# Decoder layer on one core: low score part and logits in two 64-row tiles of TensorE, one visit per pair of heads

## What is computed

```python
# 1. square-of-relu attention to 256-row weight tables, 4 heads of 64
xn = layernorm(x, g, b)
p = square(relu(einsum('bhtd,sd->bhts', heads(xn), w_fc.reshape(-1, 64))))   # 1024 keys
x = layernorm(x + x + einsum('bhts,sd->bhtd', p, w_proj.T.reshape(-1, 64)))
# 2. cross attention, 16 heads of 16, with a bias from the fractions
Q, K, V = x @ Wq.T + bq, ctx @ Wk.T + bk, ctx @ Wv.T + bv
D = clip(frac_k - frac_q, -0.2, 0.2)
attn = gamma * Q @ K.T * 0.25 + delta * (ap[h] * max(D, 0) + an[h] * min(D, 0))
x = layernorm(x + softmax(attn) @ V @ Wo.T + bo)
# 3. one of 8 low-rank experts per token, chosen by argmax of a gate, on a shared FFN
inter = relu(x @ Wi.T + wi_b + lora_expert(x))                               # 1024 wide
x = layernorm(x + inter @ Wo2.T + wo_b)
```

## Time and profile before

| | us |
|---|---|
| median of three runs (914.18 to 917.05) | 916.64 |
| the profiled execution: its own time | 914.81 |
| its span, first to last instruction | 913.0 |
| TensorE busy | 857.1 (94%) |
| VectorE busy | 778.7 (85%) |
| ScalarE busy | 690.3 (76%) |
| GpSimd busy | 533.2 (58%) |

### The profile page before, as it was taken

How to read it: one execution, slowest core, us unless ns; L and a number is a source line. 1 busy time by engine, 2 the same in 40 slices (tenths; PEclk the granted TensorE clock), 3 DMA queues, 4 the chain that set the end, 5 groups by cost and what they waited for, 6 DMA issues and landing times.

```text
span 913.0 us, 20283 instructions
## 1 busy us (share of the span) xinstructions
PE 857.1 (94%) x7140; PEld 682.6 (75%) x7140; DVE 778.7 (85%) x2286; ACT 690.3 (76%) x1453; POOL 533.2 (58%) x620
## 2 busy tenths in 40 slices
PE   2697989999999999999999999999999999999876
PEld 1344767878878787877887787887878787788666
DVE  3869989889998998989898998989899897899842
ACT  3557889788787878878787978878797887877721
POOL 2757776666656765666666666665666565533210
PEclk9989999999999999999999999999999999999998
DMA  5223322222122223122222322212222312223000
GB/s 151 87 46 68 65 47 54 36 54 41 35 48 58 54 48 64 35 44 55 39 54 58 54 44 53 45 32 51 59 54 47 64 33 32 58 38 66 14 13 23
DMA packets 40022, 46.10 MB, mean 50 GB/s; under 512 B 10257, under 2 KB 27153, under 8 KB 39922
## 3 DMA queue, kind: packets, MB, share of 16 engines
q1 hardware_dynamic: 39922, 44.82, 24.6%
HBM read 15.42 MB, written 4.19 MB: 21 GB/s over the span
## 4 chain that ended last, share of the span: by engine, by line
PE 83%; DVE 8%; ACT 3%; issue 2%; DMA 1%; POOL 1%; SPq 0%; POOLq 0%; DVEq 0%
PE bank L218 28%; PE bank L262 12%; PE bank L343 11%; PE bank L250 7%; PE bank L334 6%; PE bank L355 6%; PE bank L251 6%; PE bank L282 2%; PE bank L404 2%; DVE bank L761 2%; PE bank L365 1%; DVE T L768 1%; DVE R L717 1%; DMA STG<-in_WvT 1%; PE bank L239 1%
## 5 line engine op out<-in xcount | busy, mean ns | idle before, releaser
L964 POOL TENSOR_SCALAR U<-DP,alph 128x512 f32<-128x512 f32 x256 | 181.5, 711 | 153.6 <-DVE NM L768 92.3
L953 POOL TENSOR_TENSOR R<-R 128x512 f32<-128x512 f32 x212 | 221.9, 1052 | 78.4 <-ACT R L496 78.4
L548 ACT ACTIVATE P<-T,NM 128x256 f32<-128x256 f32 x512 | 232.0, 508 | 3.2 <-DVE NM L768 2.7
L761 DVE SCALAR_TENSOR_TENSOR bank<-DN,alph,bank 128x512 f32<-128x512 f32 x256 | 191.9, 750 | 36.7 <-PE bank L334 35.0
L475 ACT ACTIVATE STG<-bank 128x512 f32<-128x512 f32 x256 | 152.5, 596 | 70.5 <-PE bank L343 69.1
L768 DVE CUSTOM_DVE_ANT_0 T<-bank,U 128x256 f32<-128x256 f32 x512 | 197.0, 422 | 8.8
L496 ACT ACTIVATE R<-bank 128x512 f32<-128x512 f32 x256 | 151.8, 597 | 54.4 <-PE bank L251 53.3
L343 PE MATMUL bank<-ident,P 128*128 128x128 f32 x1024 | 154.6, 273 | 5.0 <-ACT STG L475 4.8
L343 PEld LDWEIGHTS bank<-ident,P 128*128 128x128 f32 x1024 | 119.3, 140 | 24.0 <-ACT P L548 8.4
L262 PE MATMUL bank<-R,VS 128*32 128x512 f32 x1024 | 124.5, 604 | 5.5 <-DVE R L717 5.2
L250 PE MATMUL bank<-SK,KH 128*128 128x512 f32 x256 | 114.9, 449 | 8.2 <-DVE SK L711 7.6
(11 more groups left out here) (165 smaller groups left out, 1863.3 us busy)
## 6 DMA issues: line engine op xcount, KB each, us to landing
QS<-QK SPq DMA_DIRECT2D x384, 64.0 KB, 2.3
XG<-in_x SPq DMA_DIRECT2D x16, 256.0 KB, 2.7
CT<-in_ctxT SPq DMA_DIRECT2D x16, 256.0 KB, 3.6
out<-XO SPq DMA_DIRECT2D x16, 256.0 KB, 2.2
FK<-in_frac SPq DMA_DIRECT2D x16, 128.0 KB, 3.5
STG<-in_wiT SPq DMA_DIRECT2D x2, 512.0 KB, 3.5
STG<-in_woT SPq DMA_DIRECT2D x2, 512.0 KB, 4.0
STG<-in_kT SPq DMA_DIRECT2D x2, 256.0 KB, 4.0
```

What stands on the lines that cost most here:

```text
L548: eng.activation(P[n % NP][:, cs], T[n % NT][:, cs], ACT.Exp, bias=NM[:, n % 8, q:q + 1], scale=-1.0).then_inc(s_ex, 1)
L761: eng.scalar_tensor_tensor(out=L[:, :], in0=dn[:, :], scalar=alph[:, 16 + h:17 + h], in1=L[:, :], op0=ALU.mult, op1=ALU.add).then_inc(s_t1, 1)
L953: eng.tensor_tensor(r[:, :], r[:, :], r[:, :], ALU.mult).then_inc(s_sqp, 1)
L964: eng.tensor_scalar(U[n % NU][:, :], dp[:, :], alph[:, h:h + 1], 0.0, ALU.mult, ALU.add).then_inc(s_u, 1)
```

## The change

The product with the low keys (`KL`) now takes only the 64 rows of its own half that hold the high activation, and the two halves h = 0 and h = 1 stand in rows 0 to 63 and 64 to 127. The restacked queries and keys of two heads share the 128 rows (rows 0 to 47 and 64 to 111), so `QS` has half the columns, needs no zeros, and the four clearing instructions on GpSimd are gone. Such a matmul uses half of the array's rows (a 64-row tile), and the two halves write to different banks. `visit(k)` takes the place of `scores` and `logits`: it issues the high products of two score units, then the four logits matmuls of two heads, then the low products of the two units. `LEAD` = 14 sets which score units go with which heads. Both banks `pL` are filled in one visit, so a visit waits until both heads of the visit before have been read (`s_tt`, 4 * k). `head` pairs the heads so that two that stand 64 rows apart come together.

Buffers: eight `R` for six, three `U` for two, seven `STG` slots for six. `due` can shift items in the first batch (`early`) and the last (`late`), and space pairs unevenly (`gap`), and nearly all of its numbers are new.

```diff
-        NR = 6
+        NR = 8
-        QS = [sb(f"QS{i}", [128, 2, 4, 256], f32r) for i in range(2)]
+        QS = [sb(f"QS{i}", [128, 2, 2, 256], f32r) for i in range(2)]
-        NU, NT, NP, NQ = 2, 3, 3, 6
+        NU, NT, NP, NQ = 3, 3, 3, 7
         def head(n):
-            return (n % 16) // 2 + 8 * (n % 2)
+            return n % 16 // 4 * 2 + n % 2 + 8 * (n % 4 // 2)
+        LEAD = 14
-        def due(g, first, count=1, step=0, start=0):
+        def due(g, first, count=1, step=0, gap=None, start=0, early=0, late=0):
             for u in range(count):
-                b, over = divmod(g - first - step * u, PERIOD)
-                if over == 0 and start <= b < NB:
+                at = g - first - (step * u if gap is None else step * (u // 2) + gap * (u % 2))
+                b, over = divmod(at - early, PERIOD)
+                if over == 0 and start <= b <= 0:
                     yield b, u
+                b, over = divmod(at, PERIOD)
+                if over == 0 and max(start, 1) <= b < NB - 1:
+                    yield b, u
+                if at == PERIOD * (NB - 1) + late:
+                    yield NB - 1, u
-            def scores(b, u):
-                c, h = unit(u)
-                bank, before = take("sc", b, u)
-                bank_free(before)
-                pe.wait_ge(s_wlo["kT"], 1)
-                pe.wait_ge(s_skl, 2 * b + 2)
-                both = SK[:, h, :, :].rearrange("p a t -> p (a t)")
-                eng.matmul(bank[:, :], KH[:, c * 128:c * 128 + 128], both, start=True, stop=False)
-                eng.matmul(bank[:, :], KL[:, c * 128:c * 128 + 128], both, start=False, stop=True).then_inc(s_sc, 1)
+            def visit(k):
+                b, c = (k + LEAD) // 8, (k + LEAD) % 8
+                if b < NB:
+                    pe.wait_ge(s_wlo["kT"], 1)
+                    pe.wait_ge(s_skl, 2 * b + 2)
+                    for h in range(2):
+                        bank, before = take("sc", b, 2 * c + h)
+                        bank_free(before)
+                        eng.matmul(bank[:, :], KH[:, c * 128:c * 128 + 128],
+                                   SK[:, h, :, :].rearrange("p a t -> p (a t)"), start=True, stop=False)
+                if k >= 0:
+                    G, m = k // 2, k % 2
+                    pe.wait_ge(d_q[G % 2], 96 * (G // 2 + 1))
+                    pe.wait_ge(s_tt, 4 * k)
+                    for q in range(2):
+                        for j in range(2):
+                            rows = slice(64 * j, 64 * j + 48)
+                            i = eng.matmul(pL[j][:, q * 256:q * 256 + 256],
+                                           QS[G % 2][rows, 0, m, q * 128:q * 128 + 128], QS[G % 2][rows, 1, m, :],
+                                           start=True, stop=True)
+                            if q == 1:
+                                i.then_inc(s_lg, 1)
+                if b < NB:
+                    for h in range(2):
+                        own = slice(64 * h, 64 * h + 64)
+                        eng.matmul(bank_of["sc", b, 2 * c + h][:, :], KL[own, c * 128:c * 128 + 128],
+                                   SK[own, h, :, :].rearrange("p a t -> p (a t)"), start=False,
+                                   stop=True).then_inc(s_sc, 1)
-            def logits(n):
-                G, L = n // 4, pL[n % 2]
-                pe.wait_ge(d_q[G % 2], 96 * (G // 2 + 1))
-                pe.wait_ge(s_tt, 2 * (n - 1))
-                for q in range(2):
-                    i = eng.matmul(L[:, q * 256:q * 256 + 256], QS[G % 2][:, 0, n % 4, q * 128:q * 128 + 128],
-                                   QS[G % 2][:, 1, n % 4, :], start=True, stop=True)
-                i.then_inc(s_lg, 1)
...
-                for b, u in due(g, -5, 16, 39):
-                    logits(16 * b + u)
+                for b, u in due(g, -26, 8, 80, start=-2):
+                    if 8 * b + u + LEAD >= 0:
+                        visit(8 * b + u)
-                for b, u in due(g, -939, 4, 141):
+                for b, u in due(g, -931, 4, 153, early=-41, late=6):
                     av(b, u)
-                for b, u in due(g, 343, 4, 140):
+                for b, u in due(g, 293, 4, 147, early=-4, late=6):
                     values(4 * b + u)
...
-                sp.wait_ge(s_qz, 4)
                 for r, (q, k) in enumerate(((1, 2), (0, 2), (1, 3))):
                     for j in range(2):
                         p = 32 * g + 16 * j
-                        dst, src = QS[s][16 * r:16 * r + 16, :, 2 * j:2 * j + 2, :], QK[p:p + 16, q:k + 1:k - q, :, :]
+                        o = 64 * j + 16 * r
+                        dst, src = QS[s][o:o + 16, :, :, :], QK[p:p + 16, q:k + 1:k - q, :, :]
```

261 lines of the change are left out of this document (126 added, 135 removed).

## The result

The changed kernel takes 943.71 us (median of 4 runs, 942.73 to 945.09) against 916.61 before: 1.0302 times as long, 95% interval 1.0287 to 1.0318. The forecast was 929 us. The direction and the range (896 to 948) held, the size didn't: 27 us slower, not 12. The profiled execution has a span of 942.4 us and a mean granted clock of 0.982 (before 913.0 and 0.992).

The account below looks back on a forecast made before the run. TensorE sets the period. Per batch -3.8 + 4.1 + 1.4 = +1.7 us, times 12 = +20.4; other batches +1.2, start -6.5, end -1.5: span 913.0 to 926.6, forecast 929 us (1.3% slower), range 896 to 948.

Parts of the forecast that it names:

- (a): TensorE: 16 low score products and 16 heads' logits become 8 pairs each, side by side: -3.8 us per batch.
- the estimate of -2.6: Halved matmuls at 77% of ideal, from the skill's 3.07 times for four row tiles; not used in the sum.
- (b): TensorE mode changes: eight visits at 0.35 us and four more column groups at 0.32: +4.1 us per batch.
- (c): TensorE waits at `uT` for VectorE's gating after `gsT`: +1.4 us per batch, bounds 0 and 2.0.
- a sign that the prediction is wrong: TensorE at L414 was to wait over 1 us for VectorE once per batch; never waiting would refute the prediction.
- The four other batches: Batches outside the steady twelve get halved matmuls and mode changes only: +0.3 us each, +1.2 us together.
- (e): Start: batch 0's fourth `av` no longer stands behind a waiting score, and all later batches follow: -6.5 us.
- (f): End: the projection of batch 15 comes one block of 12 matmuls earlier: -1.5 us, bounds 0 and -3.
- (d): Larger rings `R`, `U`, `STG`, clearing of `QS` on GpSimd and copies in `restack`: costed at nothing.
- cheap mode changes: Rival: a visit's 64-row group costs 0.15 us, not 0.35, and new waits halve to 0.7: 897 us; chance 0.27.
- the even case: Rival: mode changes cost 4.1 us per batch but new waits only 0.3: 915 us; chance 0.13.
- the serial case: Rival: the two halves don't run side by side, so halved matmuls save 0: 984 us; chance 0.08.

Follow-up runs that it names:

- a1_full_rows: Changed kernel, same order, with logits and low products as 128-row matmuls one after the other (two heads' logits summed): 951.58 us, ratio 1.0394.
- b1_rows64: Kernel before, with each low score product reading only its own 64 rows, unpaired and in place: 998.90 us, ratio 1.0911.
- c4_start: Kernel before with three moves at the start, among them batch 0's fourth `av` ahead of batch 1's first score; no 64-row tiles: 915.77 us, ratio 0.9999.
- d1_split_handover: `a1_full_rows` with a pair's second head issued 40 numbers after the first, each waiting for its own logits bank alone: 948.02 us, ratio 1.0343.
- e1_full_ends: Changed kernel with logits and low products as 128-row matmuls in batches 0, 1, 14 and 15, 64-row tiles only between: 940.27 us, ratio 1.0267.
- b3_pair_scores: Kernel before with two heads' scores in one pair, low products in 64-row tiles side by side, logits one head at a time: 982.03 us, ratio 1.0714.
- f2_rings: Changed kernel with the earlier kernel's rings (`R` 6 not 8, `U` 2 not 3, transposed P 6 not 7): 943.01 us, ratio 1.0295.
- a2_merged: Changed kernel with `values` placed right behind `av`, four column-tile groups per batch instead of eight: 1061.74 us, ratio 1.1601.

## Why the prediction was wrong, by its own steps

(a) *Halved matmuls, -3.8 us per batch.* Right: pairs start a few ns apart, a visit's four logits matmuls take 0.34 us and not 0.48, and `a1_full_rows` with the price of `b1_rows64` gives 3.7; the estimate of -2.6 beside the term doesn't come out. One sign that I had named came out otherwise: the third logits matmul starts 0.22 us behind the first, not 0.12, and the low products 0.12 behind the third. So 0.10 us of the edge lies inside the group.

(b) *More changes of mode, +4.1.* Right. A 64-row group costs 0.36 (`a1_full_rows`) or 0.35 us (`b1_rows64`), forecast 0.35; a column group 0.28 to 0.31, forecast 0.32. The measured sum is 2.88 + 1.24 = 4.1 us.

(c) *New waits, +1.4.* The size was about right, the place wrong. Of `a1_full_rows`'s 2.4 us over before, 1.24 are column groups, which leaves 1.2 for waits, now short ones of TensorE for ScalarE. That 1.2 is a remainder, not a reading. The only line that the waits of TensorE list for the changed kernel from 212 to 752 us, ten batches, gives 0.7 us per batch of them:

```profile
PE bank L378 <- ACT STG L497: 6.6, 20, 0.5
```

`uT` (L414) comes 2.07 us after `gsT` (L406), as worked out (2.04), and doesn't wait: L414 waits in none of the batches 0 to 13, which I had named as a sign that the prediction is wrong. What failed is the length of the gating, taken from the earlier trace rows as 3.40 us from `gsT`. After the change it takes 1.7. The timelines of VectorE, before and after, show two instructions that shrank:

```profile
517.07 0.17 DVE L804 TENSOR_TENSOR g<-bank,gm 128x16 f32<-128x16 f32 x1
517.28 0.84 DVE L806 TENSOR_TENSOR g<-g,dec 128x16 f32<-128x16 f32 x1
518.16 0.17 DVE L809 TENSOR_REDUCE gm<-g 128x2 f32<-128x16 f32 x1
518.36 1.13 DVE L811 TENSOR_TENSOR g<-g,gm 128x16 f32<-128x16 f32 x1
```

```profile
530.16 0.18 DVE L828 TENSOR_TENSOR g<-g,dec 128x16 f32<-128x16 f32 x1
530.37 0.17 DVE L831 TENSOR_REDUCE gm<-g 128x2 f32<-128x16 f32 x1
530.58 0.18 DVE L833 TENSOR_TENSOR g<-g,gm 128x16 f32<-128x16 f32 x1
```

And GpSimd's timeline before shows what they stood against:

```profile
516.81 1.28 POOL L946 TENSOR_TENSOR XN<-XN,gB 128x512 f32<-128x512 f32 x1
518.17 1.29 POOL L948 TENSOR_TENSOR XN<-XN,bB 128x512 f32<-128x512 f32 x1
```

L806 ends at 518.12 and L811 at 519.49, both 0.03 us behind the end of GpSimd's instruction. L804, which reads one operand from a PSUM bank, runs in the middle of the same GpSimd instruction and takes 0.17 us. In the changed kernel GpSimd is idle from 529.79 to 531.76, and the two take 0.18 us each. The kernel before shows the same by itself: in batches 0 to 11 both stand against GpSimd and take 0.84 and 1.13 us, in batches 12 to 15 GpSimd runs nothing beside them and they take 0.18. The trace before thus held the short gating too, and I had read a middle batch alone. The Trainium skill (SBUF — State Buffer, section "SBUF: two separate sides") calls the port pair that VectorE and GpSimd share an exclusive lock, which a VectorE instruction with two SBUF inputs needs too; the rows agree with that rule, as L806 and L811 have two such inputs and L804 one.

So the steady step came out near the forecast, +1.5 us per batch (forecast 1.7), by one right term, one right price and, by luck, one wait of about the right size at another place.

*The four other batches, +0.3 each: this is the first step that failed.* I gave them (a) and (b) and left out (c), as if the waits belonged to the steady stretch. They lose at least as the others do, 1.5 us each, so 6.2 instead of 1.2; in all, batches 0 and 1 lost 6.6 us and the stretch from batch 14 on 8.2. The column groups and short waits of `a1_full_rows` are there in all batches: its ends lie 2 x 2.4 + 1.1 and 2 x 2.4 + 1.5 us over before.

(e) *The start, -6.5: the second step that failed.* The fourth `av` came as forecast: it ends at 44.4 us instead of 49.9, and the residual of batch 0 starts 6.3 us earlier, at 46.17 instead of 52.42. But I had read its row wrongly. Its 3.57 us, where such a group takes 1.92, I put down to the score in front of it. The windows of the trace before show the clock instead, at 0.50 while it runs, and the timeline after shows the `av` as long again, with no score in front:

```profile
44.50:51.20 6.70, 6.08 (x21) 2.26 (x22) 3.44 (x4) 1.32 (x3) 1.84 (x1) 0.50 0.29 67
```

```profile
40.83 3.62 PE L293 MATMUL bank<-R,VS 128*32 128x512 f32 x16 [1.85 <-DVE R L739]
```

And the gain isn't kept. At the first logits 3.4 of the 6.3 us are left. After the change, TensorE stands idle for 3.56 us behind the residual and then runs the twelve matmuls of the key projection at clock 0.50, in 2.48 us instead of 1.42. The `av` behind them starts at 55.58 us, not earlier than before (55.12), and the query projection, on which the logits hang, comes only behind it. The timeline of TensorE after the change:

```profile
51.20 1.09 PE L313 MATMUL bank<-ident,X 128*128 128x128 f32 x4 [3.56 <-ACT X L531]
```

The key projection in the critical chain, after and before:

```profile
52.29 2.48 PE bank L230 x12
```

```profile
58.93 1.42 PE bank L218 x12
```

Nor is what is left at the first logits kept by later batches. `c4_start` gains 2.7 us there and has 0.7 left at batch 2: its batch 0 takes 41.3 us at clock 0.92, where before it was 39.2 at 1.00. The step treated the `av` as the head of a chain that moves all batches. The joint handover adds to it in the changed kernel: 1.4 us in batch 0 at equal clock (`d1_split_handover`).

*The clock: no step had it.* Stretches at half clock cost the changed kernel, beyond what full rows cost in matmul time, 2.2 + 2 x 0.9 = 4.0 us in batches 0 and 1 and 0.9 + 2 x 0.9 = 2.7 us from batch 14 on (`e1_full_ends` against after, with 0.9 us per batch from `a1_full_rows`). The ends of `a1_full_rows` run the same instructions as those of `e1_full_ends`, and the same reckoning with them gives 0.7 + 1.8 = 2.5 and 1.9 + 1.8 = 3.7 us; so far apart lie two profiled executions. The sums may also share some us with the handover, since waits and clock come together. The profile before showed a clock of 0.95 behind the last L754 and of 0.50 from 44.5 to 51.2 us, which should have made it a rival.

(f) *The end, -1.5: failed.* From the last logits to the end it is 53.9 us after and 53.8 before. Of the 9.1 us by which this stretch missed the forecast, 2.5 are the two batches at their steady price, 2.7 to 3.7 the clock, 1.5 the absent gain; 1.4 to 2.4 stay open. `d1_split_handover` gives nothing back here and `b3_pair_scores` loses nothing, which speaks against the handover of the logits banks and the pair of scores as their cause. Batch 14 has a wait that no middle batch has and the kernel before hasn't either; `a1_full_rows` has it too, so it comes with the order. Waits of TensorE from 803.3 to 851.7 us:

```profile
PE bank L230 <- DVE X2L L753: 1.5, 1, 1.5
```

What is left as a cause is the order of the last batch (the `late` numbers), which wasn't tried.

(d) *Nothing for the rings:* right (`f2_rings`).

The rivals: cheap mode changes fall by (b), the even case by (c), where some 1.2 and not 0.3 is left, the serial case by (a).

## What to carry to other kernels

Price a change of tile mode per group and count the groups; here the count and a price of 0.28 to 0.36 us gave the +4.1 us per batch that was forecast. A pair of low products saves 0.23 us and a group costs 0.35, so 64-row tiles pay here only because logits worth another 0.24 share the group. They did pay, by 0.9 us per batch; what made the kernel slower is the order that came with them, 2.4 us per batch by `a1_full_rows`. Give the batches at the ends the whole steady price, and look at the granted clock of a row before reading its length as a wait. Where the length of a chain of small instructions on VectorE decides, look at GpSimd's timeline, in every batch, before taking it as fixed.

## What was not expected of the hardware

- A 128x16 `tensor_tensor` of VectorE with both inputs in SBUF took 0.84 or 1.13 us beside a GpSimd `tensor_tensor` and 0.18 without.
- A kernel with 3.8 us more matmul work and eight changes of mode less per batch at its ends, which by the middle batches should cost 0.9 us, is 3.4 us faster (940.27 against 943.71), with a mean clock of 0.989 instead of 0.982 to 0.985.
- A 64-row group costs 0.35 us among 128-row matmuls (`b1_rows64`), in the mean 0.14 on the way in and 0.20 on the way out, and two logits matmuls that stand 64 rows apart start 3 to 5 ns apart.
- Moving eight column-tile groups per batch by 28 to 37 of 640 numbers, and one copy with them, made the kernel 118 us slower (`a2_merged`), more than any edit of the tiles.
